# Token rows of the second-to-last stored pair gathered instead of multiplied in, in a fused attention and expert kernel on one core

## The chip, the core and the metric

The kernel runs on one core of a Trainium2 chip. The metric is device time in microseconds, the median of several executions. The kernel before takes 277.7 us (three runs, 277.69 to 277.87). Its times below come from one further execution, taken with the profiler: 277.88 us as timed, of which the profile's span covers 276.1 us, with a granted TensorE clock of 0.998.

The engines are TensorE (PE; its weight loads are listed as PEld), VectorE (DVE), ScalarE (ACT), GpSimd (POOL), and SyncE (SP), which only issues DMAs here. Each engine takes its instructions in the order of the program and stops at a semaphore wait.

## What is computed

Two blocks with a residual each, over 16 batches of 128 tokens with 256 features (2048 tokens):

```
x = x + xattn(layernorm(x), ctx)        # per batch: causal 128 keys + 128 context keys
    h      = layernorm(x);  normed = rmsnorm(h) * norm_w;  pool = [normed, ctx]
    attn   = softmax(mask((normed Wq)(pool Wk)^T / 16))
    alpha  = sigmoid(h Wg + b)
    result = (1 - alpha) * h + alpha * (attn pool)
x = x + ffn(layernorm(x))               # 8 experts, 512 token slots each, top_idx
    for e in 0..7:  rows = layernorm(x)[top_idx[:, e]]                 # 512 x 256
                    out[top_idx[:, e]] += (gelu(rows W1[e] + b1) W2[e] + b2) * combine_w
```

All of it is float32. The large products are made in three passes over a high and a low part (`x_hi`, `x_lo`, `w_hi`, `w_lo`), each held in TensorE's fp32r format.

## The kernel before, in words

**First stage, attention.** The 16 batches are worked in 8 pairs (0 to 7). Every engine runs `attention(p)` once per pair. PE makes the logits, the gate product, the transposes of the probabilities (L1228) and the product with the values (L1244). DVE masks the logits (L901), forms the difference to h (L849), mixes it with the gate (L857, called `mix`), adds the residual to get `x2` (L864), and makes the statistics for the second layernorm. POOL adds x + h ahead of time (`x_plus_h`, L494), makes `normed` (L453) and the inverse root (`rstd`, L471). ACT writes the normalised rows `xn2` (L620). SP stores `x2` to the output (L383) and `xn2` to the table `token_rows` in DRAM.

**Second stage, experts.** For expert e the 512 rows of its slots are gathered from `token_rows` by four indirect DMAs of 128 rows each, which POOL issues (tiles 0 to 3). PE transposes them into two PSUM banks (`ps_xT`), ACT copies them out as `x_hi` (L712), DVE forms `x_lo` (L1021). Then come 8 up products and 8 down products, with gelu on ACT (L731, L732) and its low part on DVE (L1073). While expert e runs, ACT and DVE also split the next expert's weights (L737, L1078). DVE further makes four slot totals per expert (L1052: which slots name the same token), which need the table `seen`. POOL writes `seen` once, after the gathers for expert 1 (L533): a memset (L554) and four selects (L557).

**The seam between the two.** Expert 0 must not wait until the last pairs' rows have gone to DRAM and come back. So its rows come in two parts that are summed in `ps_xT`:

- rows of the first pairs are stored, gathered (`gather_first_rows`, L473), and added by a product with the identity (`early_rows`, L1256). Rows of the late pairs stand as zeros in the table at that time, so that the gather brings zeros for them.
- rows of the late pairs are multiplied in from SBUF by one-hot matrices (`late_rows`, L1264), once with their high and once with their low part. A one-hot matrix (128 x 512) per late batch says which slot wants which token; DVE makes them during the attention stage (`one_hot`, L881).

`EARLY_PAIRS` (L54) is the number of pairs that go by gather. In the kernel before it is 5, so pairs 5, 6 and 7 go by one-hot products: 6 one-hot matrices and 24 products of 128 x 512. The operands are in three slots: `late_hi[0]`, `late_lo[0]` for pair 5 (in the storage of M, free by then), slot 1 for pair 6 (in that of the gate weight), slot 2 for pair 7.

The zeros would be lost if a late pair's rows were stored before the first gathers have read the table. SP therefore waits for all four of them (L400, L401) before it stores the late pairs, and after these come the last list of indices (L407), `x2` of pair 7 (L383) and the two halves of pair 7's rows (L393). POOL's gathers for expert 1 wait until all these stores have landed (L550, L551).

## Time and profile before

| | kernel before |
|---|---|
| median of 3 runs | 277.7 us |
| profiled execution | 277.88 us, span 276.1 us |
| PE busy | 266.3 us (96%) |
| DVE busy | 222.7 us (81%) |
| ACT busy | 180.1 us (65%) |
| POOL busy | 161.7 us (59%) |
| attention stage ends, first rows of expert 0 transposed | about 83.4 us |
| chain that ended last, by engine | PE 81%, DVE 8%, issue 4%, POOL 3%, ACT 2%, DMA 1% |

Times in the rows are microseconds from the start of the span. Busy time does not count waits. A row of the timeline shows the start, the duration from the first start to the last end, the engine, the line, the operation with its output and inputs, and in brackets the idle time ahead of it with what ended it. Consecutive instructions of an engine overlap by some 0.1 us, since the next starts while the last is draining.

### The profile page before, as it was taken

How to read it: one execution, taken by the hardware profiler on the slowest of the kernel's cores; microseconds unless marked ns; L12 is line 12 of the kernel's file. 1: busy time of each engine (PE TensorE's matmuls, PEld its weight loads, DVE VectorE, ACT ScalarE, POOL GpSimd, SP SyncE). 2: the span in 40 equal slices, each digit the busy share in tenths (PEclk: the TensorE clock that was granted, in tenths of full speed). 3: DMA queues.
4: the chain of work that ended last, by engine and by line, in shares of the span. 5: the costliest groups of instructions: out<-in, count | busy, mean ns of one | idle time of the engine just before them, and what ended most of it. 6: DMA issues, size and time to landing. Idle time of an engine off the chain costs nothing.

```text
span 276.1 us, 5494 instructions
## 1 busy us (share of the span) xinstructions
PE 266.3 (96%) x1698; PEld 237.0 (86%) x1698; DVE 222.7 (81%) x526; ACT 180.1 (65%) x341; POOL 161.7 (59%) x153
## 2 busy tenths in 40 slices
PE   6899999999989999999999999999999999999992
PEld 2689899999866989989899899899899899999992
DVE  1988999899986599978878797797887979777552
ACT  2688899886767765766666658567575675763540
POOL 4475766656835945647556457655645746604555
PEclk9999999999999999999999999999999999999999
DMA  6993258496564755635554544654446451100021
GB/s 199 358 275 100 87 143 226 129 260 225 160 197 131 286 153 157 198 117 170 154 200 147 142 141 140 188 174 138 153 133 199 155 156 69 57 21 33 34 78 69
DMA packets 30293, 42.45 MB, mean 154 GB/s; under 512 B 5251, under 2 KB 24015, under 8 KB 30148
## 3 DMA queue, kind: packets, MB, share of 16 engines
q1 hardware_dynamic: 25392, 30.00, 34.7%
q0 software_dynamic: 4608, 12.24, 14.9%
q8 instruction: 8, 0.13, 0.2%
q14 instruction: 9, 0.07, 0.1%
q10 hardware_dynamic: 276, 0.00, 0.1%
HBM read 33.54 MB, written 9.24 MB: 155 GB/s over the span
## 4 chain that ended last, share of the span: by engine, by line
PE 81%; DVE 8%; issue 4%; POOL 3%; ACT 2%; DMA 1%; DVEq 0%; POOLq 0%; ACTq 0%
PE bank L1155 22%; PE bank L1157 22%; PE bank L1156 22%; PE bank L1199 3%; PE bank L1244 3%; PE bank L1296 2%; PE bank L1315 1%; PE bank L1319 1%; PE bank L1316 1%; DMA x_all<-in_x_dram 1%; POOL out_dram L546 1%; DVE bn L754 1%; PE bank L1151 1%; PE bank L1228 1%; PE bank L1164 1%
## 5 line engine op out<-in xcount | busy, mean ns | idle before, releaser
L731 ACT ACTIVATE keysT<-bank,biasT 128x512 f32<-128x512 f32 x63 | 43.5, 690 | 65.4 <-PE bank L1157 55.0
L546 POOL DMA_INDIRECT out_dram<-h,sidx x32 | 38.5, 1205 | 37.5 <-DVE h L1045 30.5
L537 POOL DMA_INDIRECT x_all<-out_dram,idx_all x32 | 39.4, 1232 | 24.3 <-DMA out_dram<-h,sidx 16.8
L1155 PE MATMUL bank<-x_hi,w_hi 128*128 128x512 f32 (+1 forms) x114 | 45.2, 397 | 0.0
L1157 PE MATMUL bank<-x_hi,w_lo 128*128 128x512 f32 (+1 forms) x114 | 44.2, 388 | 0.0
L1156 PE MATMUL bank<-x_lo,w_hi 128*128 128x512 f32 (+1 forms) x114 | 44.1, 387 | 0.0
L533 POOL DMA_INDIRECT x_all<-token_rows,idx_all x28 | 29.8, 1066 | 19.2 <-DVE factor L1096 8.7
L1052 DVE SCALAR_TENSOR_TENSOR junk<-idx_rows,idx_f,normed 128x512 bf16<-128x512 bf16 (+1 forms) x32 | 38.6, 1206 | 3.0 <-POOL normed L557 3.0
L1078 DVE TENSOR_TENSOR w_lo<-w_raw,w_hi 128x512 fp32r<-128x512 f32 x56 | 38.4, 685 | 0.0
L1157 PE MATMUL bank<-w_hi,g_lo 128*128 128x256 f32 x128 | 36.2, 283 | 0.0
L1156 PE MATMUL bank<-w_lo,g_hi 128*128 128x256 f32 x128 | 36.2, 283 | 0.0
L1155 PE MATMUL bank<-w_hi,g_hi 128*128 128x256 f32 x128 | 36.1, 282 | 0.0
L1073 DVE TENSOR_TENSOR g_lo<-keysT,g_hi 128x512 fp32r<-128x512 f32 x32 | 22.1, 690 | 17.1 <-ACT g_hi L732 17.1
L737 ACT CAST w_hi<-w_raw 128x512 fp32r<-128x512 f32 x56 | 34.7, 619 | 0.0
L1157 PEld LDWEIGHTS bank<-x_hi,w_lo 128*128 128x128 f32 x114 | 21.4, 188 | 4.8
L1155 PEld LDWEIGHTS bank<-w_hi,g_hi 128*128 128x128 f32 x128 | 24.4, 190 | 1.3
L1156 PEld LDWEIGHTS bank<-w_lo,g_hi 128*128 128x128 f32 x128 | 24.4, 190 | 1.2
L1157 PEld LDWEIGHTS bank<-w_hi,g_lo 128*128 128x128 f32 x128 | 24.4, 190 | 0.0
L1155 PEld LDWEIGHTS bank<-x_hi,w_hi 128*128 128x128 f32 x114 | 21.5, 189 | 2.8 <-ACT g_hi L732 0.4
L1156 PEld LDWEIGHTS bank<-x_lo,w_hi 128*128 128x128 f32 x114 | 21.6, 189 | 2.4
L732 ACT ACTIVATE g_hi<-bank,biasT 128x512 fp32r<-128x512 f32 x32 | 21.8, 682 | 0.0
L1157 PE MATMUL bank<-w_hi,gateT_lo 128*128 128x256 f32 x64 | 18.0, 282 | 0.0
(172 smaller groups left out, 713.1 us busy)
## 6 DMA issues: line engine op xcount, KB each, us to landing
w_raw<-in_L_ffn_W_dram SPq DMA_DIRECT2D x32, 512.0 KB
idx_rows<-in_L_ffn_top_idx_dram SPq DMA_DIRECT2D x8, 256.0 KB, 4.1
out_dram<-x SPq DMA_DIRECT2D x8, 256.0 KB, 3.0
hn_cnat<-in_ctx_dram SPq DMA_DIRECT2D x7, 256.0 KB, 2.8
token_rows<-xn SPq DMA_DIRECT2D x7, 256.0 KB, 2.2
hn_cnat<-in_L_ffn_b_dram SPq DMA_DIRECT2D x1, 1024.0 KB, 6.6
x_all<-in_x_dram SPq DMA_DIRECT2D x3, 256.0 KB, 4.6
x_all<-in_x_dram SPq DMA_DIRECT2D x1, 768.0 KB, 8.3
```

What stands on the lines that cost most here:

```text
L533: g.indirect_dma_start(xg[:, s, t, :], None, rows_dram, list_of(e, t)).then_inc(xg_in[s], 16)
L537: g.indirect_dma_start(accg[:, t, :], None, flat, list_of(e, t)).then_inc(acc_in[t], 16)
L546: g.indirect_dma_start(flat, idx(sidx[:, t:t + 1].bitcast(U32), 0), newrow[:, t, :], None, bounds_check=N - 1, oob_is_err=False).then_inc( ...
L731: a.activation(g32[:, f % NG, :], ps_up[f % 2][:, :], ACT.Gelu_apprx_tanh, bias=bias)
L732: a.activation(g_hi[f % NG], ps_up[f % 2][:, :], ACT.Gelu_apprx_tanh, bias=bias).then_inc(g_rdy, 1)
L737: a.copy(w_hi[:, 1 - s, col], w_raw[:, col]).then_inc(whi_rdy, 1)
L1052: v.scalar_tensor_tensor(junk[:, :], rows_by_expert[:, ds(e, 1), :].rearrange("p a c -> p (a c)"), idx_f[:, ds(t * NE + e, 1)], seen[:, t, ...
L1073: v.tensor_tensor(g_lo[f % NG], g32[:, f % NG, :], g_hi[f % NG].bitcast(F32), ALU.subtract)\
L1078: v.tensor_tensor(w_lo[:, 1 - s, col], w_raw[:, col], w_hi[:, 1 - s, col].bitcast(F32), ALU.subtract).then_inc(wlo_rdy, 1)
L1155: t_.matmul(dst, lhs_hi, rhs_hi, start=first, stop=False)
L1156: t_.matmul(dst, lhs_hi, rhs_lo, start=False, stop=False)
L1157: return t_.matmul(dst, lhs_lo, rhs_hi, start=False, stop=last_one)
```

## The change

Pair 5 joins the pairs that are stored and gathered: `EARLY_PAIRS` becomes 6, so there are 4 one-hot matrices instead of 6, and two slots of operands instead of three. The cast and the subtraction that made pair 5's high and low part are gone, and so are its 8 products. Two products with a matrix of zeros (`junk`) now open the accumulation in `ps_xT` instead. They stand in the last pair behind the transposes of the probabilities.

The four first gathers wait for pair 5's store. All of them now stand behind the last pair's x + h on POOL: tiles 0 and 1 ahead of `rstd` of pair 6, tile 2 ahead of the last pair's first `rstd`, tile 3 ahead of its second. On PE the products of the seam are in a new order, and DVE makes the low part of the last pair's first batch ahead of the last shift.

```diff
-    EARLY_PAIRS = NPAIR - 3
+    EARLY_PAIRS = NPAIR - 2
...
-        late_hi = [M_hi[:, :, :], gateT_hi[:, :, :], hnT_hi[:, 0, :, :]]
-        late_lo = [M_lo[:, :, :], gateT_lo[:, :, :], hnT_lo[:, 0, :, :]]
+        late_hi = [gateT_hi[:, :, :], hnT_hi[:, 0, :, :]]
+        late_lo = [gateT_lo[:, :, :], hnT_lo[:, 0, :, :]]
...
-                    for late in (LAST - 2, LAST - 1):
-                        sp.wait_ge(xn_rdy, 2 * late + 2)
-                        sp.dma_start(rows_v[:, 2 * late:2 * late + 2, 0:H], xn2[:, late % 2, :, :])\
-                            .then_inc(xn_out[late % 2], 16)
+                    sp.wait_ge(xn_rdy, 2 * r + 2)
+                    sp.dma_start(rows_v[:, 2 * r:2 * r + 2, 0:H], xn2[:, r % 2, :, :]).then_inc(xn_out[r % 2], 16)
...
                 if is_last(p):
-                    gather_first_rows(range(1, NT))
+                    gather_first_rows(range(2))
...
-                if p == LAST - 1:
-                    gather_first_rows(range(1))
...
             for b in range(2):
+                gather_first_rows(range(2 + b, 3 + b))
                 last_rstd(b)
...
-                if is_last(p):
-                    act.wait_ge(xn_rdy, 2 * p - 2)
-                    act.wait_ge(q_mm, NPAIR)
-                    a.copy(late_hi[0], xn2[:, s, :, :]).then_inc(late_hi_rdy, 1)
                 for b in range(2):
...
-                    a.copy(late_hi[1], xn2[:, 1 - s, :, :]).then_inc(late_hi_rdy, 1)
+                    a.copy(late_hi[0], xn2[:, 1 - s, :, :]).then_inc(late_hi_rdy, 1)
...
-                a.activation(late_hi[2][:, b, :], x2[:, 1, b, :], ACT.Identity, bias=shift2[:, 1, b:b + 1],
+                a.activation(late_hi[1][:, b, :], x2[:, 1, b, :], ACT.Identity, bias=shift2[:, 1, b:b + 1],
...
-                    if not is_last(p):
+                    if not isinstance(p, int):
...
                 v.reciprocal(rinv[:, :], rsum[:, :]).then_inc(ri_rdy, 1)
-                if is_last(p):
-                    dve.wait_ge(late_hi_rdy, 1)
-                    dve.wait_ge(xn_rdy, 2 * LAST - 2)
-                    v.tensor_tensor(late_lo[0], xn2[:, s, :, :], late_hi[0].bitcast(F32), ALU.subtract)\
-                        .then_inc(late_lo_rdy, 1)
...
             last_pair_variance(1)
-            dve.wait_ge(late_hi_rdy, 2)
+            dve.wait_ge(late_hi_rdy, 1)
...
-            v.tensor_tensor(late_lo[1], xn2[:, 1 - last_s, :, :], late_hi[1].bitcast(F32), ALU.subtract)\
+            v.tensor_tensor(late_lo[0], xn2[:, 1 - last_s, :, :], late_hi[0].bitcast(F32), ALU.subtract)\
                 .then_inc(late_lo_rdy, 1)
+            def last_pair_low(b):
+                dve.wait_ge(late_hi_rdy, 2 + b)
+                dve.wait_ge(last_xn[b], 1)
+                v.tensor_tensor(late_lo[1][:, b, :], xn_last[:, b, :], late_hi[1][:, b, :].bitcast(F32),
+                                ALU.subtract).then_inc(late_lo_rdy, 1)
+            last_pair_low(0)
             last_pair_shift(1)
...
-            for b in range(2):
-                dve.wait_ge(late_hi_rdy, 3 + b)
-                dve.wait_ge(last_xn[b], 1)
-                v.tensor_tensor(late_lo[2][:, b, :], xn_last[:, b, :], late_hi[2][:, b, :].bitcast(F32),
-                                ALU.subtract).then_inc(late_lo_rdy, 1)
+            last_pair_low(1)
...
-                    pe.wait_ge(log_rdy, 2 * NPAIR - 1)
-                    pe.wait_ge(late_hi_rdy, 1)
-                    for b in range(2):
-                        late_rows(0, b, late_hi, first=b == 0)
                 pe.wait_ge(exp_rdy, 2 * p + 2)
...
                 if is_last(p):
-                    early_rows(range(1))
+                    pe.wait_ge(log_rdy, 2 * NPAIR - 1)
+                    for k in range(KH):
+                        t_.matmul(ps_xT[k][:, :], junk[:, 0:P], junk[:, :], start=True, stop=False)
...
-            def late_rows(n, b, part, first=False):
+            def late_rows(n, b, part):
...
-                              start=first, stop=False)
+                              start=False, stop=False)
             each_pair(pe, attention)
-            early_rows(range(1, NT))
-            for n in range(2):
-                if n:
-                    pe.wait_ge(late_hi_rdy, n + 1)
-                    for b in range(2):
-                        late_rows(n, b, late_hi)
-                pe.wait_ge(late_lo_rdy, n + 1)
+            early_rows(range(2))
+            pe.wait_ge(late_hi_rdy, 1)
+            for b in range(2):
+                late_rows(0, b, late_hi)
+            early_rows(range(2, 3))
+            pe.wait_ge(late_hi_rdy, 2)
+            late_rows(1, 0, late_hi)
+            pe.wait_ge(late_lo_rdy, 1)
+            for b in range(2):
+                late_rows(0, b, late_lo)
+            early_rows(range(3, NT))
+            for k in range(KH):
+                cols = slice(k * P, (k + 1) * P)
+                pe.wait_ge(late_hi_rdy, 3)
+                t_.matmul(ps_xT[k][:, :], late_hi[1][:, 1, cols], onehot[:, 3, :], start=False, stop=False)
                 for b in range(2):
-                    late_rows(n, b, late_lo)
-            for b in range(2):
-                pe.wait_ge(late_hi_rdy, 3 + b)
-                late_rows(2, b, late_hi)
-            for k in range(KH):
-                for b in range(2):
-                    pe.wait_ge(late_lo_rdy, 3 + b)
-                    last = t_.matmul(ps_xT[k][:, :], late_lo[2][:, b, k * P:(k + 1) * P], onehot[:, 4 + b, :],
+                    pe.wait_ge(late_lo_rdy, 2 + b)
+                    last = t_.matmul(ps_xT[k][:, :], late_lo[1][:, b, cols], onehot[:, 2 + b, :],
```

POOL at the seam, kernel before (from the last `rstd` inside the loop of pairs; `rstd ... 128x2` is a pair's, `128x1` one batch's of pair 7; `x_all<-token_rows` are gathers, the first four for expert 0, the last for expert 1):

```order
L471 TENSOR_TENSOR rstd<-var_eps,half_neg 128x2 [waits x2_var_eps_ready]
L481 DMA x_all<-token_rows,idx_all 128x264 [waits xn2_stored0,late_rows_zeroed,xn2_stored1,idx_loaded,combine_copied]
L494 TENSOR_TENSOR x_plus_h<-x_all,h 128x512 [waits x2_shift_ready,h_ready]
L481 DMA x_all<-token_rows,idx_all 128x264 [waits xn2_stored0,late_rows_zeroed,xn2_stored1,idx_loaded,combine_copied]
L481 DMA x_all<-token_rows,idx_all 128x264 x2
L471 TENSOR_TENSOR rstd<-var_eps,half_neg 128x2 [waits x2_var_eps_ready]
L523 TENSOR_TENSOR rstd<-var_eps,half_neg 128x1 [waits x2_var_eps_ready] x2
L533 DMA x_all<-token_rows,idx_all 128x264 [waits xn2_stored1,x2_stored1,x2_stored0,xn2_stored0]
```

The same place on POOL in the changed kernel:

```order
L469 TENSOR_TENSOR rstd<-var_eps,half_neg 128x2 [waits x2_var_eps_ready]
L492 TENSOR_TENSOR x_plus_h<-x_all,h 128x512 [waits x2_shift_ready,h_ready]
L479 DMA x_all<-token_rows,idx_all 128x264 [waits xn2_stored0,late_rows_zeroed,xn2_stored1,idx_loaded,combine_copied]
L479 DMA x_all<-token_rows,idx_all 128x264
L469 TENSOR_TENSOR rstd<-var_eps,half_neg 128x2 [waits x2_var_eps_ready]
L479 DMA x_all<-token_rows,idx_all 128x264 [waits xn2_stored0,late_rows_zeroed,xn2_stored1,idx_loaded,combine_copied]
L519 TENSOR_TENSOR rstd<-var_eps,half_neg 128x1 [waits x2_var_eps_ready]
L479 DMA x_all<-token_rows,idx_all 128x264 [waits xn2_stored0,late_rows_zeroed,xn2_stored1,idx_loaded,combine_copied]
L519 TENSOR_TENSOR rstd<-var_eps,half_neg 128x1 [waits x2_var_eps_ready]
L530 DMA x_all<-token_rows,idx_all 128x264 [waits xn2_stored1,x2_stored1,x2_stored0,xn2_stored0]
```

The last pair's x + h has moved ahead of the gathers, and the gathers of tiles 2 and 3 now stand each in front of one of the last pair's inverse roots.

PE in the last pair, kernel before (behind the gate product; `w_hi` holds the one-hot matrices, `M_hi` pair 5's high part, L1228 transposes the probabilities, L1261 is a gathered tile):

```order
L1219 MATMUL bank<-ident,bias_rows 128x64 [waits bias_loaded]
L1268 MATMUL bank<-w_hi,M_hi 128x512 [waits one_hot_ready,late_rows_high,masked_logits_max]
L1268 MATMUL bank<-w_hi,M_hi 128x512
L1268 MATMUL bank<-w_hi,M_hi 128x512 [waits one_hot_ready]
L1268 MATMUL bank<-w_hi,M_hi 128x512
L1228 MATMUL bank<-ident,setup_or_probs 128x128 [waits exp_done]
L1228 MATMUL bank<-ident,setup_or_probs 128x128 x3
L1261 MATMUL bank<-ident,x_all 128x128 [waits first_rows_gathered0]
L1261 MATMUL bank<-ident,x_all 128x128
L1244 MATMUL bank<-normed,setup_or_probs 128x256 [waits diff_ready,normed_ready,probsT_ready]
```

The same place on PE in the changed kernel:

```order
L1211 MATMUL bank<-ident,bias_rows 128x64 [waits bias_loaded]
L1216 MATMUL bank<-ident,setup_or_probs 128x128 [waits exp_done]
L1216 MATMUL bank<-ident,setup_or_probs 128x128 x3
L1225 MATMUL bank<-junk 128x512 [waits masked_logits_max]
L1225 MATMUL bank<-junk 128x512
L1234 MATMUL bank<-normed,setup_or_probs 128x256 [waits diff_ready,normed_ready,probsT_ready]
```

The transposes of the probabilities follow the gate product directly, and tile 0 of the gathered rows has moved behind the product with the values.

## Rows read from the trace of the kernel before

**Rows 1.** busy time of each engine (instructions) in one stretch of expert 0.

```profile
100.00:110.00 10.00, 10.00 (x65) 8.99 (x64) 9.93 (x21) 6.38 (x12) 4.42 (x5) 1.00 0.52 144
```

**Rows 2.** chain of waits, in order of time: start, us, what; the seam.

```profile
83.45 0.59 ACT x_hi L712
```

**Rows 3.** timeline of PE, end of attention.

```profile
71.94 1.20 PE L1268 MATMUL bank<-w_hi,M_hi 128*128 128x512 f32 x4
72.98 0.60 PE L1228 MATMUL bank<-ident,setup_or_probs 128*128 128x128 f32 x4
...
74.26 0.70 PE L1244 MATMUL bank<-normed,setup_or_probs 128*128 128x256 f32 x2 [0.23 <-ACT setup_or_probs L653]
```

**Rows 4.** timeline of ACT, last pair.

```profile
69.44 1.09 ACT L620 ACTIVATE xn<-x,shift,rstd 128x256 f32<-128x256 f32 x2 [1.30 <-DVE shift L888]
70.56 0.62 ACT L642 CAST M_hi<-xn 128x512 fp32r<-128x512 f32 x1
...
73.62 0.59 ACT L653 COPY setup_or_probs<-bank 128x512 f32<-128x512 f32 x1 [1.44 <-PE bank L1228]
```

**Rows 5.** timeline of DVE, pairs 6 and 7.

```profile
63.75 0.48 DVE L883 TENSOR_SCALAR w_hi<-idx_rows,tok_f 128x512 fp32r<-128x512 f32 x1
...
70.92 1.52 DVE L857 SCALAR_TENSOR_TENSOR diff<-setup_or_probs,diff 128x512 f32<-128x512 f32 x1
...
75.12 0.67 DVE L948 TENSOR_TENSOR M_lo<-xn,M_hi 128x512 fp32r<-128x512 f32 x1
75.71 0.48 DVE L966 SCALAR_TENSOR_TENSOR diff<-bank,rinv,h 128x256 f32<-128x256 f32 x1
...
77.03 0.15 DVE L888 SCALAR_TENSOR_TENSOR shift<-mv,rstd 128x2 f32<-128x2 f32 x1
```

**Rows 6.** all instructions of L857: duration in ns, min/median/max.

```profile
L857 DVE SCALAR_TENSOR_TENSOR diff<-setup_or_probs,diff x7: 682/684/1518, 25.9 to 70.9; 128x512 f32<-128x512 f32 x7
```

**Rows 7.** timeline of POOL, last pair and after.

```profile
69.35 1.21 POOL L481 DMA_INDIRECT x_all<-token_rows,idx_all  x1 [0.20 <-issue]
70.58 1.30 POOL L494 TENSOR_TENSOR x_plus_h<-x_all,h 128x512 f32<-128x512 f32 x1
...
74.83 0.95 POOL L481 DMA_INDIRECT x_all<-token_rows,idx_all  x1 [0.30 <-issue]
75.80 0.73 POOL L471 TENSOR_TENSOR rstd<-var_eps,half_neg 128x2 f32<-128x2 f32 x1
78.05 0.56 POOL L523 TENSOR_TENSOR rstd<-var_eps,half_neg 128x1 f32<-128x1 f32 x1 [1.51 <-DVE var_eps L985]
...
85.05 1.04 POOL L533 DMA_INDIRECT x_all<-token_rows,idx_all  x1 [3.86 <-DMA token_rows<-qT]
...
92.42 2.32 POOL L557 TENSOR_SCALAR_AFFINE_SELECT normed<-normed 128x512 bf16<-128x512 bf16 x4
```

**Rows 8.** timeline of SP, DMAs issued at the seam.

```profile
77.94 0.87 SPq L404 DMA_DIRECT2D token_rows<-xn  x2
...
79.41 0.46 SPq L383 DMA_DIRECT2D out_dram<-x  x1
80.02 2.17 SPq L393 DMA_DIRECT2D token_rows<-qT  x2
```

**Rows 9.** DMA issues of 77 to 86 us: KB each, median us to landing.

```profile
token_rows<-xn SPq DMA_DIRECT2D x2, 256.0 KB, 2.4
...
out_dram<-x SPq DMA_DIRECT2D x1, 256.0 KB, 4.0
token_rows<-qT SPq DMA_DIRECT2D x2, 128.0 KB, 2.9
```

**Rows 10.** timeline of DVE in expert 0.

```profile
94.88 1.24 DVE L1052 SCALAR_TENSOR_TENSOR junk<-idx_rows,idx_f,normed 128x512 bf16<-128x512 int32 x1 [2.98 <-POOL normed L557]
...
104.86 1.28 DVE L1021 TENSOR_TENSOR x_lo<-bank,x_hi 128x512 fp32r<-128x512 f32 x2
```

**Rows 11.** timeline of the weight loads, start of expert 1.

```profile
106.19 0.19 PEld L1319 LDWEIGHTS bank<-x_lo,w_hi 128*128 128x128 f32 x1 [0.16 <-issue]
```

More of the change, by code:

```diff
@@ L386, in _ @@
                     load_ctx(r + 3)
-                if r == EARLY_PAIRS - 2:
+                if r == EARLY_PAIRS - 3:
                     sp.wait_ge(xh_rdy, r + 1)
```

## The prediction

> **What bounds the kernel now.** I read the table of stretches first. While the experts run, PE has no gap: in the stretch from 100 to 110 us it is busy 10.00 of 10.00 us, and DVE 9.93 [rows 1]. So what the seam gives or takes reaches the end in full, if PE still starts expert 0 at the seam's pace and nobody makes it wait later. The chain of waits says when expert 0's rows are ready: ACT starts to copy them at 83.45 [rows 2]. That is the time the change works on. Then I looked for whoever has no slack in expert 0, and it is DVE. It stands still for 2.98 us until POOL has written `seen` (its first slot total starts at 94.88), and from there it works without a pause to the low parts of expert 1's rows, L1021, which end at 104.86 + 1.28 = 106.14 [rows 10]. PE's weight load that needs them starts at 106.19, after 0.16 us of idling [rows 11]. PE itself doesn't stall there, since the matmuls in front of it still run, so the slack of this second chain is 0.05 to 0.15 us; I take 0.1. Read backwards it is: x_lo of expert 1, DVE's block of work, `seen` (selects end at 92.42 + 2.32 = 94.74), POOL's memset and gathers for expert 1 from 85.05, and these waited 3.86 us for the last store of pair 7's rows to land [rows 7]. The forecast is decided on this chain, not on the one that the change shortens.
>
> **PE, ACT and DVE in the last pair.** The four products between the gate product and the transposes go: 72.98 - 71.94 = 1.04 us [rows 3]. ACT's cast L642 (0.62, of which some 0.5 is its place in the queue) goes with them, so the second exponential ends near 71.65 and doesn't hold the transposes back [rows 4]. The evacuation L653 moves from 73.62 to about 72.6 and the product with the values from 74.26 to 73.2. The two products with zeros lie in the gap that PE has while ACT evacuates (0.23 us idle before 74.26, and tile 0 has left it) [rows 3, 4]: two at the 0.3 us of a 512-column product (1.20 for four) fit into the 0.6 us of the evacuation, cost 0.
>
> On DVE, L857 took 1.52 us in the last pair and 0.684 in the median of seven [rows 5, 6]. It began at 70.92, while POOL's x + h ran from 70.58 to 71.88 [rows 7]. 71.88 + 0.6 is its end, so it looks as if it worked only after POOL was done. In the new order x + h stands ahead of the gathers and starts near 69.3, as soon as pair 5's shift is out. It ends by 70.6, before L857, and 0.83 us come back. L948 (75.12 to 75.71, 0.59) goes as well [rows 5]. DVE would be free for the last pair's difference L966 at 75.71 - 0.83 - 0.59 = 74.29; the values come about 1.04 earlier than before, near 74.5. I take 74.5: 1.2 us won. The one-hot matrices of pairs 5 and 6 (0.4 each by their place in the queue, 63.75 [rows 5]) leave DVE too. PE is dense there, so this moves nothing but pair 5's statistics, 0.4 us sooner.
>
> The Trainium skill bears on L857 ("SBUF — State Buffer", the section on the single rule): a DVE instruction with two SBUF inputs and a POOL instruction that reads SBUF take turns for a whole instruction. The two rows fit it. If that rule were not the cause, L857 would stay at 1.52 and the sum below would be 0.8 us worse.
>
> **POOL: the gathers.** Here is what the change costs. Before, tile 0 was issued at 69.35 and tile 3 at 74.83 [rows 7]. Now the first one waits for pair 5's rows. ACT wrote them from 69.44 for 1.09 us, to 70.5 [rows 4]; with 0.4 from the one-hot matrix, 70.1. Their store takes 2.4 us to land [rows 9], POOL 0.3 us from a landing to the next gather (SP's last store was issued at about 81.8, its row's end 80.02 + 2.17 less an issue of some 0.4 [rows 8], and landed 2.9 later at 84.7; POOL starts at 85.05). That makes 72.8 for tile 0, 3.4 us later than before. Two gathers of 1.05 + 0.3 end at 75.2, `rstd` of pair 6 (0.73) at 75.95. DVE wants it for the shift that stood 1.32 us behind L966 (75.71 to 77.03 [rows 5]): at 75.8 in the new kernel. It waits 0.2 and goes on at 76.0. Tile 2 runs from 76.15 to 77.2. The last pair's first `rstd` was issued 1.02 us behind that shift (78.05 [rows 7]), and now runs from 77.2 to 77.8. Tile 3 follows at 77.95, which is 3.1 us later than 74.83.
>
> **PE at the seam.** SP's first store behind the gathers was issued 3.11 us after tile 3 (77.94 [rows 8] less 74.83), so tile 3 is there at 81.05. PE then has one tile (four blocks, 0.5) and three products of 512 columns (1.20 for four [rows 3], so 0.9): ACT starts at 82.5 instead of 83.45 [rows 2]. Expert 0 begins 0.95 us sooner. The DVE part alone would allow 82.2.
>
> **SP and POOL behind it.** SP's queue is what ties the two chains. It may not store pair 6 before tile 3 is there. From 81.05 it issues pair 6's store (0.44, half of 0.87), the last list (79.41 - 77.94 - 0.87 = 0.60), `x2` (0.5) and pair 7's first half (0.4), so its second half is issued at 82.95 [rows 8]. Before, that was at 81.8, when it waited for DVE and not for the queue. So it is 1.15 us later. It lands 2.9 us after its issue [rows 9], or more, because the four DMAs ahead of it (256 + 256 + 256 + 128 KB) are now all issued within 2 us; the store of `x2` took 4.0 in the crowd before [rows 9], which bounds it at +1.1. I take 0.15 of that. POOL starts expert 1's gathers 1.3 us late, at 86.35, and `seen` is ready at 96.05 in place of 94.74.
>
> **The sum.** DVE's block moves with `seen`: x_lo is ready at 107.45. Less the slack of 0.1, PE is 1.2 us later than before at the start of expert 1, whatever it won at 82.5. (It stalls in two steps: first for the low part of gelu 3, which DVE makes right behind the first slot total, then for x_lo.) From there PE is dense in both kernels and nothing is given back. 277.88 + 1.2 = 279.1 for an execution like the profiled one, which is 0.18 above the median of the three; against that median it is 278.9.
>
> **Bounds.** The least delay: the store lands so soon that gathers never hold up DVE's shift. Then the shift is at 75.8, tile 3 at 77.7, landing as before at 2.9: +0.7, 278.4. The most: L857 keeps its 1.52 (+0.8) and the last store takes 4.0 (+0.9): 280.6. Indirect DMAs cost 0.95 to 1.21 each in the rows [rows 7], so three of them carry 0.8 between the ends; I took the middle.
>
> **Rivals.** *Faster:* the seam alone decides and POOL's and SP's later queue is covered. Then PE keeps its 0.95 us, or 1.25 if tile 3 comes sooner: 276.4 to 276.8. For it: the chain of the profile runs through DVE and PE at the seam, never through SP. Against it: DVE's 2.98 us wait for `seen` is in the rows, and x_lo has no slack. It needs the last store issued by 81.8, hence tile 3 by 76.8; POOL would have to issue it ahead of an inverse root whose input DVE has at about 76.9.
>
> *No change:* the last store catches up most of the way. Its landing in the crowd before (2.9 us with a list and an `x2` ahead) may already hold 0.5 to 1 us of queueing that doesn't grow. With 1.15 reduced to 0.3 to 0.6 the result is 277.7 to 278.2.
>
> *Slower by more:* pair 5's store lands late. It is the front of DVE's chain as well: each 0.1 us later than 72.5 moves tiles 0 and 1, pair 6's `rstd`, DVE's shift and everything behind it, with no slack (DVE waits 0.2 already). A landing of 4.0, the largest of the rows [rows 9], instead of 2.4 gives +1.6: 280.5. Against it: SP issues nothing else for some microseconds ahead of it.
>
> A rule that bears on this landing: by the Trainium skill ("DMA: Bandwidth & Descriptors", the anatomy of one DMA), about 2.0 us of a DMA is fixed and mostly the receipt of the last write. With 2.0 for pair 5's store in place of 2.4 the delay would be 0.2 us less, not more, since DVE sets the rest.
>
> **Chances.** Slower along this chain, 278.3 to 279.6: 0.57. Slower by more: 0.15. No change: 0.15. Faster: 0.13. A measurement of this kernel tells a change above about 0.2%, 0.55 us, from none. So slower 0.72, same 0.15, faster 0.13. The time of the likeliest case is 278.9. The range 277.4 to 280.3 leaves out most of the faster case and the upper third of the last.
>
> **What would show it.** In the new trace: L857 of the last pair at 0.68; the product with the values near 73.2; the first gather near 72.8 with an idle time ended by a store, and DVE's shift of pair 6 ended by POOL's `rstd`; tile 3 issued near 78; ACT's x_hi near 82.5; SP's last row store issued near 83 and POOL's first gather for expert 1 near 86.3. The first slot total would start near 96.2, with DVE waiting 4 us or more for `seen`. PE, gapless from 84 us on before, would now show idle time between 96 and 108 us, ended by DVE. The forecast is wrong if that idle time is missing, or if the last store is issued at 82 or sooner.

## The result and the profile after

The changed kernel takes 284.1 us (four runs, 282.31 to 285.45), against 277.78 us for the kernel before in the same session (four runs, 277.69 to 279.12): ratio 1.0206, 95% interval 1.0169 to 1.0242. Slower was right. The size was not: 278.9 was predicted, with a range that ended at 280.3.

Page of the changed kernel, the profiled execution of 285.42 us: span, busy times, and the row of the slot totals, whose last field is the idle time ahead of them:

```profile
span 283.6 us, 5473 instructions
PE 269.9 (95%) x1692; PEld 238.5 (84%) x1692; DVE 221.8 (78%) x523; ACT 179.8 (63%) x340; POOL 161.1 (57%) x153
L1044 DVE SCALAR_TENSOR_TENSOR junk<-idx_rows,idx_f,normed 128x512 bf16<-128x512 bf16 (+1 forms) x32 | 38.5, 1203 | 6.5 <-POOL normed L554 6.5
```

DVE now waits 6.5 us for `seen`, where it waited 2.98 [rows 10]. But that isn't the whole loss, and it pays to cut the span at two instructions that both kernels have: the last pair's logits on PE (start: 68.49 before, 72.95 after) and the first product with `x_hi` (84.19 before, 88.23 after). Kernel before:

```profile
68.49 1.89 PE L1199 MATMUL bank<-keysT,qT 128*128 128x256 f32 x8
84.19 0.47 PE L1315 MATMUL bank<-x_hi,w_hi 128*128 128x512 f32 x1 [0.30 <-ACT x_hi L712]
```

Changed kernel:

```profile
72.95 1.89 PE L1191 MATMUL bank<-keysT,qT 128*128 128x256 f32 x8
88.23 0.47 PE L1307 MATMUL bank<-x_hi,w_hi 128*128 128x512 f32 x1
```

| | before | after | difference |
|---|---|---|---|
| start of span to last pair's logits | 68.49 | 72.95 | +4.46 |
| logits to first product with x_hi ("seam") | 15.70 | 15.28 | -0.42 |
| from there to the end ("rest") | 191.91 | 195.37 | +3.46 |
| span | 276.1 | 283.6 | +7.5 |

**The first part** lies ahead of everything that the change touches. PE at the start, changed kernel (start, us, instruction, idle time ahead):

```profile
1.33 4.02 PE L1122 MATMUL bank<-junk 128*128 128x512 bf16 x9 [1.33 <-POOL junk L425]
7.05 2.08 PE L1131 MATMUL bank<-setup_or_probs 128*128 128x256 f32 x4 [1.70 <-DMA setup_or_probs<-in_L_xattn_k_w_dram]
9.78 1.91 PE L1131 MATMUL bank<-setup_or_probs 128*128 128x256 f32 x4
```

and in the kernel before:

```profile
6.12 1.13 PE L1139 MATMUL bank<-setup_or_probs 128*128 128x256 f32 x4 [0.77 <-DMA setup_or_probs<-in_L_xattn_k_w_dram]
8.25 1.03 PE L1139 MATMUL bank<-setup_or_probs 128*128 128x256 f32 x4
```

The k weights landed 0.93 us later, and then the same four products took 2.08 us instead of 1.13, the next four 1.91 instead of 1.03: about half speed, as the clock's lower level of 1.2 GHz in place of 2.4 would give, although the column of the granted clock says 1.00 there. It lasts until about 16.5 us, and with the 0.93 us off it costs some 3.5 us.

**The other two parts** are the change. To compare with the rows of before, take 4.46 off each time (68.49 against 72.95 for the last pair's logits). SP, changed kernel:

```profile
74.62 0.36 SPq L396 DMA_DIRECT2D token_rows<-xn  x1
86.16 0.36 SPq L403 DMA_DIRECT2D token_rows<-xn  x1
86.57 0.48 SPq L343 DMA_DIRECT2D idx_rows<-in_L_ffn_top_idx_dram  x1
87.09 0.45 SPq L383 DMA_DIRECT2D out_dram<-x  x1
87.58 0.96 SPq L393 DMA_DIRECT2D token_rows<-qT  x2
```

POOL, the same stretch:

```profile
77.79 1.21 POOL L479 DMA_INDIRECT x_all<-token_rows,idx_all  x1 [2.96 <-DMA token_rows<-xn]
80.27 0.78 POOL L469 TENSOR_TENSOR rstd<-var_eps,half_neg 128x2 f32<-128x2 f32 x1
83.06 1.12 POOL L479 DMA_INDIRECT x_all<-token_rows,idx_all  x1 [0.17 <-issue]
92.81 1.00 POOL L530 DMA_INDIRECT x_all<-token_rows,idx_all  x1 [7.60 <-DMA token_rows<-qT]
```

Four rows of the chain of waits (start, us, what) show what lies between a store's issue and the gather that waits for it. "issue" is POOL starting its DMA after the landing:

```profile
74.62 2.25 DMA token_rows<-xn
76.93 0.86 issue
88.09 3.88 DMA token_rows<-qT
92.10 0.71 issue
```

POOL's gathers for expert 1 start at 92.81 - 4.46 = 88.35, against 85.05 [rows 7]: 3.3 us later, not 1.3. DVE (the mix of the last pair is L850 now, the difference L954, pair 6's shift L881):

```profile
75.38 0.69 DVE L850 SCALAR_TENSOR_TENSOR diff<-setup_or_probs,diff 128x512 f32<-128x512 f32 x1
79.07 0.48 DVE L954 SCALAR_TENSOR_TENSOR diff<-bank,rinv,h 128x256 f32<-128x256 f32 x1
81.09 0.16 DVE L881 SCALAR_TENSOR_TENSOR shift<-mv,rstd 128x2 f32<-128x2 f32 x1 [0.62 <-POOL rstd L469]
102.57 1.19 DVE L1044 SCALAR_TENSOR_TENSOR junk<-idx_rows,idx_f,normed 128x512 bf16<-128x512 int32 x1 [6.52 <-POOL normed L554]
```

And PE, which in the kernel before stands still for 0.2 to 0.4 us at a time in the seam and nowhere from 85 us on:

```profile
77.73 0.70 PE L1234 MATMUL bank<-normed,setup_or_probs 128*128 128x256 f32 x2 [0.24 <-ACT setup_or_probs L646]
81.60 1.21 PE L1251 MATMUL bank<-ident,x_all 128*128 128x128 f32 x8 [1.88 <-DMA x_all<-token_rows,idx_all]
100.78 1.09 PE L1288 MATMUL bank<-ident,x_all 128*128 128x128 f32 x8 [0.66 <-DMA x_all<-token_rows,idx_all]
104.43 0.39 PE L1147 MATMUL bank<-w_hi,M_lo 128*128 128x256 f32 x1 [1.17 <-DVE gateT_lo L1065]
113.16 1.09 PE L1311 MATMUL bank<-x_lo,w_hi 128*128 128x512 f32 x2 [0.47 <-DVE x_lo L1013]
```

The first gathered tiles in the kernel before:

```profile
77.13 1.41 PE L1261 MATMUL bank<-ident,x_all 128*128 128x128 f32 x8 [0.27 <-DMA x_all<-token_rows,idx_all]
```

PE stands still in the seam for 1.88 us for the first gathered tiles. Behind it, it waits for the low part of gelu 3 (1.17 us) and for x_lo of expert 1 (0.47 us, and 0.90 us for the weight load), as forecast from the late `seen`. The wait of 0.66 us for expert 1's gathered rows is not in the forecast. It doesn't set the end here, since DVE's chain is later still, but after_sp below is left with it.

### The profile page after: what moved, and what is told of

Its sections match the earlier page's. It is cut to its first block, busy times and chain, and to the rows that moved or that the text cites. A ratio compares the mean times of both kernels' runs of the same rounds, so it can differ in the third digit from the quotient of the medians.

```text
span 283.6 us, 5473 instructions
## 1 busy us (share of the span) xinstructions
PE 269.9 (95%) x1692; PEld 238.5 (84%) x1692; DVE 221.8 (78%) x523; ACT 179.8 (63%) x340; POOL 161.1 (57%) x153
## 4 chain that ended last, share of the span: by engine, by line
PE 74%; DVE 6%; POOL 6%; DMA 5%; issue 4%; ACT 2%; SPq 1%; DVEq 0%; POOLq 0%; ACTq 0%
PE bank L1147 20%; PE bank L1149 19%; PE bank L1148 19%; PE bank L1191 4%; PE bank L1234 2%; DMA setup_or_probs<-in_L_xattn_k_w_dram 2%; PE bank L1288 2%; DVE junk L1044 2%; POOL x_all L530 2%; DMA token_rows<-qT 1%; PE bank L1131 1%; PE bank L1311 1%; PE bank L1143 1%; POOL x_all L479 1%; DMA x_all<-token_rows,idx_all 1%
## 5 line engine op out<-in xcount | busy, mean ns | idle before, releaser
L534 POOL DMA_INDIRECT x_all<-out_dram,idx_all x32 | 38.8, 1213 | 23.5 <-DMA out_dram<-h,sidx 16.0
L1147 PE MATMUL bank<-w_hi,M_lo 128*128 128x256 f32 x64 | 18.1, 283 | 1.2 <-DVE gateT_lo L1065 1.2
```

The lines of the kernel that those rows point to most:

```text
L534: g.indirect_dma_start(accg[:, t, :], None, flat, list_of(e, t)).then_inc(acc_in[t], 16)
L1147: t_.matmul(dst, lhs_hi, rhs_hi, start=first, stop=False)
```

## The experiments

All times are medians in us; "seam + rest" is from the last pair's logits to the end of the span in the profiled execution, which leaves the start out (before: 207.61, after: 210.65). Executions of the kernel before itself fall into two groups, near 277.7 and near 279.1; before_cold below points to what sets them apart. How many fall in the upper one changed from session to session (4 of 17 to 20 of 35), so the ratios of different sessions can't be set against each other, and I read medians beside them. The expectations call two ideas by name. "Chain theory": the last row store holds POOL, POOL's late `seen` holds DVE, and DVE holds PE. "Port theory": an instruction of DVE stands still while one of POOL runs.

| run | median (runs) | ratio, 95% | seam + rest |
|---|---|---|---|
| after_again | 280.96 (5) | 1.0106, 1.0085 to 1.0126 | 210.67 |
| before_warm | 278.04 (12) | 0.9991, 0.9975 to 1.0007 | 207.62 |
| after_warm | 281.44 (5) | 1.0120, 1.0095 to 1.0145 | 210.99 |
| after_seen | 279.26 (11) | 1.0041, 1.0022 to 1.0060 | 208.67 |
| after_sp | 278.34 (12) | 0.9995, 0.9973 to 1.0017 | 208.24 |
| after_seen_wait | 278.83 (12) | 1.0010, 0.9987 to 1.0033 | 208.64 |
| after_seen_wait_sp | 279.10 (12) | 1.0021, 0.9998 to 1.0044 | 208.47 |
| before_xh | 278.78 (12) | 1.0000, 0.9978 to 1.0021 | 208.07 |
| before_cold | 279.36 (12) | 1.0042, 1.0021 to 1.0064 | 208.21 |
| before_sp | 277.86 (12) | 0.9975, 0.9958 to 0.9992 | 207.55 |
| before_probs | 278.02 (12) | 0.9984, 0.9967 to 1.0000 | 207.59 |
| after_sp_b2 | 278.09 (12) | 0.9994, 0.9975 to 1.0013 | 208.50 |
| after_sp_b2_fill | 278.15 (12) | 1.0003, 0.9982 to 1.0025 | 207.88 |
| after_cold | 282.96 (6) | 1.0199, 1.0150 to 1.0248 | 210.96 |

**after_again**: the changed kernel as it is, once more.

> The changed kernel unaltered, for more executions. Start theory: its executions fall into groups, set by when the first weights land; where TensorE idles about 1.7 us after its warm-up products, the next 9 us of products run at half speed and the execution takes about 285.4; where it idles 0.8 us, it takes 281 to 282.5. The kernel before shows the same two starts, more rarely. Rival, the change is the whole cause: all executions of the changed kernel lie at 282 to 285.5 and none of the kernel before leaves 277.7 to 277.9.

280.96 (280.64 to 281.14). All five lie at or just under the faster of the two groups that I expected (281 to 282.5); neither the slower one near 285.4 nor the rival's 282 to 285.5 was seen. PE starts the setup at 6.24 at full speed, and the last pair's logits start at 68.23. So the slow start doesn't belong to the changed kernel as such, and the change's own cost is about 3.1 us (210.67 - 207.61). Its first gather for expert 1:

```profile
88.16 1.00 POOL L530 DMA_INDIRECT x_all<-token_rows,idx_all  x1 [7.59 <-DMA token_rows<-qT]
```

**before_warm, after_warm**: 15 warm-up products instead of 9 in either kernel.

```diff
-            keep_warm(9)
+            keep_warm(15)
```

> Kernel before with 15 warm-up products in place of 9, so that TensorE works until about 6.7 us. Start theory: 277.7 to 278.0, all executions within 0.5 us, since the late landing of the first weights no longer meets an idle TensorE. Rival, the start has no part in it: the same spread as the kernel before.

> Changed kernel with 15 warm-up products. Start theory plus the chain over the last row store, POOL and DVE: the profile showed the seam's chain 3.1 us later than before beyond the start's 4.46, so 280.8, narrow. Rival, the change is the whole cause: 282 to 285.5 as without it. My forecast's size for the chain (1.2 us) would give 279.0.

No execution of before_warm lies above 278.44. The difference between the two is 3.4 us, with after_warm 0.6 us above what I expected. The profile of after_warm (mean clock 0.992, as in two more of the five) shows one more way in which a late `seen` costs. Table of stretches, PE alone: busy us (instructions), granted clock, DMA share, GB/s:

```profile
96.00:100.00 4.00, 2.18 (x14) 1.00 0.04 9
100.00:104.00 4.00, 3.93 (x18) 0.66 0.65 210
104.00:108.00 4.00, 4.00 (x26) 0.91 0.55 171
```

After PE has stood still for 1.89 us (98.2 to 100.1, for the low part of gelu 3), the granted clock is 0.50 from about 101.3 to 104.3, its lower level. So the 3.4 us hold some 0.3 us of this fall (seam + rest is 210.99, in after_again 210.67).

**after_seen**: `seen` (memset and selects) is written ahead of POOL's wait for the last store; 15 warm-up products in this and in the runs that follow, where nothing else is said.

```diff
-            for s in range(2):
-                pool.wait_ge(xn_out[s], 16 * (NPAIR // 2) + 16 + 16 * s)
-                pool.wait_ge(x2_out[s], 16 * (NPAIR // 2) + 16)
-            gather_rows(1, 1)
             pool.wait_ge(pv_mm, NPAIR)
             g.memset(seen, 1.0).then_inc(consts, 1)
...
+            for s in range(2):
+                pool.wait_ge(xn_out[s], 16 * (NPAIR // 2) + 16 + 16 * s)
+                pool.wait_ge(x2_out[s], 16 * (NPAIR // 2) + 16)
+            gather_rows(1, 1)
```

> Changed kernel with 15 warm-up products, and POOL writes the table seen ahead of its wait for the last row store instead of behind expert 1's gathers. Chain theory: DVE no longer waits 6.5 us in expert 0, what is left is expert 1's gathered rows, which TensorE needed 0.7 us before they landed; 277.9 to 278.3. Rival, another part of the change costs the time (stores, gathers or products at the seam): stays within 0.5 us of the kernel with 15 warm-up products alone.

DVE no longer waits for `seen`, and 2.2 us of the 3.4 come back. That is less than the 3.1 to 3.5 that I expected, since the memset collides with DVE in the seam:

```profile
81.21 1.68 DVE L1006 TENSOR_SCALAR qT<-x,rstd,shift 128x256 f32<-128x256 f32 x1
```

```profile
80.94 1.79 POOL L547 MEMSET normed<- 128x2048 bf16 x1
```

L1006 took 0.41 us in the changed kernel and 1.68 here: it ends (82.89) right behind POOL's memset (80.94 + 1.79 = 82.73). x_hi is 1.2 us later. The Trainium skill ("SBUF — State Buffer", Who interferes with whom) says that a DVE instruction in a mode that uses both port pairs, which tensor_scalar can enter, and a POOL instruction exclude each other for whole instructions. The trace fits that. It doesn't show in which mode L1006 ran: its 0.41 us is also what a tensor_tensor of this size takes (L1000, 0.42).

**after_sp**: `seen` stays where the change has it, and SP issues pair 7's two halves ahead of the last list and of `x2`, for which POOL's gathers no longer wait.

```diff
                 sp.wait_ge(x2_rdy, r + 1)
+                if r == LAST:
+                    for b in range(2):
+                        sp.wait_ge(last_xn[b], 1)
+                        sp.dma_start(rows_v[:, 2 * r + b, 0:H], xn_last[:, b, :]).then_inc(xn_out[r % 2], 16)
+                    sp.wait_ge(onehot_rdy, NB - EARLY)
+                    load_lists(IDX_PARTS - 1)
                 sp.dma_start(out_v[:, 2 * r:2 * r + 2, :], x2[:, r % 2, :, :]).then_inc(x2_out[r % 2], 16)
...
                 pool.wait_ge(xn_out[s], 16 * (NPAIR // 2) + 16 + 16 * s)
-                pool.wait_ge(x2_out[s], 16 * (NPAIR // 2) + 16)
             gather_rows(1, 1)
+            for s in range(2):
+                pool.wait_ge(x2_out[s], 16 * (NPAIR // 2) + 16)
```

> Changed kernel with 15 warm-up products; SP issues both halves of pair 7's rows directly behind pair 6's store, then the last list, then x2, and POOL waits for the x2 stores only behind expert 1's gathers. Chain theory: last row store issued about 1 us sooner and landing in 3 us in place of 3.9, so expert 1's gathers, seen, DVE's block and the end all 1.9 us sooner than with the warm-up alone: 279.4. Rival, the order and the crowd on SP's queue do not matter and the landing is fixed: at most 1 us, 280.4 or more. Rival, the chain doesn't end in seen: no change, 281.4.

278.34: 3.1 us of the 3.4 are gone, more than the 2 us expected. By seam + rest it is 2.4 us of the change's own 3.1 (210.67 to 208.24); 0.6 us are left, and PE's wait for the gathered rows (0.71 us) is what the profile shows for them. POOL's first gather for expert 1, the first row that PE waits for behind the seam, and the two row stores' time from issue to landing:

```profile
85.44 1.09 POOL L530 DMA_INDIRECT x_all<-token_rows,idx_all  x1 [4.69 <-DMA token_rows<-qT]
```

```profile
96.40 1.09 PE L1289 MATMUL bank<-ident,x_all 128*128 128x128 f32 x8 [0.71 <-DMA x_all<-token_rows,idx_all]
```

```profile
DMA to landing us min/median/max: 2.1/2.1/2.1
```

In the changed kernel the same two stores took

```profile
DMA to landing us min/median/max: 3.5/3.7/3.9
```

So a 128 KB store lands in 2.1 us with 256 KB of pair 6's rows issued 0.5 us ahead of it, and in 3.5 to 3.9 us with a list and an `x2` (256 KB each) in between. What is issued ahead of it makes the difference of up to 1.8 us. The Trainium skill ("DMA: Bandwidth & Descriptors", Anatomy of one DMA) puts the fixed part of a DMA that GpSimd issues at about 2.0 us, with the time of the bytes on top. By its sum the 256 KB of pair 5's store would take 2.6 us, an estimate (the prediction took the fixed part alone); the store landed in 2.25. These stores are issued by SP, and before_sp below has the same 128 KB landing in 1.7 us, so for them the fixed part is smaller than that.

**after_seen_wait, after_seen_wait_sp**: `seen` ahead of POOL's wait, but behind a wait for the last low part (so that it can't collide with L1006); the second one with SP's order too.

```diff
             pool.wait_ge(pv_mm, NPAIR)
+            pool.wait_ge(late_lo_rdy, 3)
             g.memset(seen, 1.0).then_inc(consts, 1)
```

> Changed kernel with 15 warm-up products; POOL writes seen ahead of its wait for the last row store, but only once DVE has made the last low part at the seam. Port theory: L1006 at 0.41 in place of 1.68 us and x_hi 1.2 us sooner than with seen written at once. Chain theory for the end: expert 1's gathered rows come as late as there and now bound TensorE, so 279.2 again, with TensorE idle 1.4 us ahead of their transposes. Rival, the seam alone counts once seen is out of the way: 278.0.

> Both edits together: seen early but behind DVE's last low part, and pair 7's rows stored ahead of the last list and x2. Chain theory: neither seen nor expert 1's rows bind, the seam's gain of 0.4 us stays: 277.2 to 277.6, the first version below the kernel before. Rival, some third wait of expert 0 takes over: 278.0 or more.

The port theory holds in both: the tensor_scalar is back at 0.41 us. In after_seen_wait_sp:

```profile
81.02 0.41 DVE L1008 TENSOR_SCALAR qT<-x,rstd,shift 128x256 f32<-128x256 f32 x1
```

The times are a miss in both. after_seen_wait has 278.83 instead of 279.2, and its profiled execution (279.69) has PE waiting 0.16 us for expert 1's rows instead of 1.4: it lost the time in the seam (16.46 us), where the granted clock is 0.50 from 79 to 82 us. The pair doesn't add up: together 279.10, SP's order alone 278.34. `seen` in front costs POOL about 2 us (gathers for expert 1 at 87.55 instead of 85.44), and what then ends last is no longer `seen` but the gathered rows: PE waits 0.89 us at 96.59 for them. Of after_seen_wait_sp's 12 executions 4 lie near 280.1, with a mean clock of 0.991.

**before_xh**: the kernel before, with the last pair's x + h ahead of all four gathers.

```diff
                 if is_last(p):
-                    gather_first_rows(range(1, NT))
+                    gather_first_rows(range(NT))
...
-                if p == LAST - 1:
-                    gather_first_rows(range(1))
```

> Kernel before with 15 warm-up products and only the last pair's x + h moved ahead of all four first gathers. Port theory: L857 of the last pair takes 0.68 in place of 1.52 us. The last pair's difference then starts when the values are there, 0.25 us sooner; the end doesn't move (277.9 to 278.1), since DVE's block in expert 0 starts at seen, which is as late as before. Rival, what is won at the seam reaches the end: 277.2 to 277.8. Rival, L857 is not held by POOL: stays 1.52.

The mix of the last pair takes 0.76 us instead of 1.52 [rows 5], with nothing else moved on DVE: what held it was POOL's x + h. But tile 0 is gathered 1.6 us later (2.47 us behind the last pair's logits, 0.84 in before_warm), and stands in front of the product with the values on PE, so the gain turns into a wait. DVE:

```profile
71.36 0.76 DVE L855 SCALAR_TENSOR_TENSOR diff<-setup_or_probs,diff 128x512 f32<-128x512 f32 x1
76.60 0.48 DVE L964 SCALAR_TENSOR_TENSOR diff<-bank,rinv,h 128x256 f32<-128x256 f32 x1 [1.12 <-PE bank L1242]
```

PE:

```profile
74.89 0.71 PE L1259 MATMUL bank<-ident,x_all 128*128 128x128 f32 x4 [0.86 <-DMA x_all<-token_rows,idx_all]
```

The seam is 16.14 us (15.70), the rest 191.93 (191.91): 0.44 us lost in this execution, and the median is 0.74 us above before_warm. So I was right on L857 and wrong on the time, which I had expected unchanged.

**before_probs**: in the kernel before, the transposes of the probabilities ahead of pair five's four products.

```diff
-                    pe.wait_ge(log_rdy, 2 * NPAIR - 1)
-                    pe.wait_ge(late_hi_rdy, 1)
-                    for b in range(2):
-                        late_rows(0, b, late_hi, first=b == 0)
...
                 if is_last(p):
+                    pe.wait_ge(log_rdy, 2 * NPAIR - 1)
+                    pe.wait_ge(late_hi_rdy, 1)
+                    for b in range(2):
+                        late_rows(0, b, late_hi, first=b == 0)
                     early_rows(range(1))
```

> The kernel before with 15 warm-up products, and in the last pair the transposes of the probabilities ahead of pair five's four products on PE; nothing else is moved. Theory of the seam (expert 0 starts with the last pair's statistics, through DVE): the values come 0.9 us sooner, L857 keeps its 1.5 us and DVE comes to the difference at 74.9 instead of 75.5, so x_hi is 0.5 to 0.6 us sooner than 83.66 and the time 277.5. Rival (DVE is the bound there and takes nothing sooner, or PE has the four products back at the end of the seam): 278.0 as before_warm.

278.02, seam 15.72: the rival holds. L857 still takes 1.54 and pair five's low part 0.67, and DVE comes to the difference at 75.65 as before. In the seam PE waits for DVE. That an earlier product with the values counts once L857 is short and the low part gone, as in the changed kernel, follows from this but was not run by itself.

**before_sp**: SP's order in the kernel before.

> The kernel before with 15 warm-up products and SP's order of after_sp: rows of pairs 5 and 6, both halves of pair 7, the last list, x2. Theory (expert 0 of the kernel before is bound by PE alone, and the last store already lands 2.3 us behind its issue because it waits for DVE and not for the queue): SP's order gives POOL at most 0.3 us and PE nothing: 277.8 to 278.3, the same as before_warm (278.04). Rival (SP's order shortens something else, the crowd of 80 to 98 us): 0.5 us or more faster, 277.5 or less, and then what after_sp won was not the changed kernel's own queue.

277.86 and seam + rest 207.55: the same as before_warm. Pair 7's two stores, from issue to landing:

```profile
DMA to landing us min/median/max: 1.7/1.7/1.7
```

So SP's order isn't a gain of its own; it repairs what the change broke. (The ratio, 0.9975, comes from the 20 of 35 executions of the kernel before that were in the upper group in that session.)

**before_cold, after_cold**: 5 warm-up products.

```diff
-            keep_warm(9)
+            keep_warm(5)
```

> The kernel before with 5 warm-up products instead of 9, so that PE stands idle for about 2.5 us (0.77 before) until the k weights are there. Theory of the start: an idle PE of 1.7 us or more ahead of the setup products leaves the products behind it at half speed until about 16.5 us, as in the first execution of the changed kernel (12 query products 0.21 apart, M_rows 2.08 us for four), and everything behind is 3.5 us later: 281 to 282, in all of its executions. Rival: the half speed has nothing to do with the idle time (it is only the later landing of the weights in some executions): the products start when the weights land, 277.7 to 278.4 as for 15 warm-up products.

> The changed kernel with 5 warm-up products instead of 9. In before_cold every execution was 1.2 us or more above the kernel before's lower group (products at half speed to about 10 us). Theory: the first session's times of the changed kernel (282.31, 282.78, 285.42, 285.45) are its own 280.9 and a slow start of either 1.3 or 4.5 us; then all executions here lie near 282.2, and single ones near 285.4. Rival (the slow start is of that session or the first build and not of the idle PE): 280.9 to 281.2 as in after_again.

PE at the start of before_cold:

```profile
6.19 2.08 PE L1139 MATMUL bank<-setup_or_probs 128*128 128x256 f32 x4 [2.55 <-DMA setup_or_probs<-in_L_xattn_k_w_dram]
8.91 1.29 PE L1139 MATMUL bank<-setup_or_probs 128*128 128x256 f32 x4
```

All 12 executions lie between 278.94 and 281.34, at the upper group's time or more, so products at half speed behind an idle PE are the likely cause of that group (none of its executions was profiled). But they run slow only to about 10 us, and the last pair's logits start at 69.39, 0.9 us late, not 3.5 as I expected. (The rest is 0.6 us longer too in this execution, 192.51; I found no cause.) In the changed kernel it gives 282.44 to 283.13 in four executions, 284.05, and one of 286.36. That resembles the first session's times (282.31, 282.78, 285.42, 285.45), of which only the 285.42 was profiled. What makes the slow stretch last until 16 us in some executions I haven't found.

**after_sp_b2, after_sp_b2_fill**: after_sp with the 1 MB load of the output biases later; and with five products with zeros in PE's gap ahead of the first tiles.

```diff
             sp.wait_ge(pv_mm, NPAIR)
+            sp.wait_ge(wlo_rdy, 3)
             row_broadcast(b2_bc, b2.rearrange("e h -> (e h)")).then_inc(b2_in, 16)
...
             each_pair(pe, attention)
+            for n in range(5):
+                t_.matmul(ps_xT[n % KH][:, :], junk[:, 0:P], junk[:, :], start=False, stop=False)
             early_rows(range(2))
```

(The last two lines with a + are in after_sp_b2_fill alone.)

> after_sp, and the 1 MB load of the output biases waits for the third low part of expert 1's weights: issued near 91.8 instead of 86.7, behind the gathers for expert 1. In after_sp PE stood idle 0.71 us ahead of 96.40 for the last of these gathers (issued 89.38, landed about 96.2) and 3.70 of 4.00 us busy before that. Theory (the gathers share the DMA engines with that load): they land 2 us or more sooner, the idle time goes, 277.5 to 277.8, and the executions near 279.2 with a clock of 0.992 go too. Rival (the gathers are bound by themselves or by the weights): the idle time stays, 278.3.

> after_sp_b2 with five more products with zeros on PE ahead of the first gathered tile, where PE stood idle for 1.16 to 1.5 us. Theory: the executions of the changed kernel and its variants near 279.5 (3 of 12 in after_sp, 3 of 12 in after_sp_b2, mean clock 0.992) come from the idle time that the later gathers leave in the seam: the profile of after_sp_b2 shows the granted clock at 0.50 from 79 to 82 us and a seam of 16.46 us instead of 15.32. With the gap filled none of the 12 executions has a mean clock under 0.995, and all lie at 277.8 to 278.5. Rival (that clock falls for another reason): 2 to 4 of 12 near 279.5 again. A price of up to 0.1 us where a zero product stands in front of tile 0.

PE's wait at 96.4 is gone in both, but the median of after_sp_b2 is 278.09, only 0.25 us less and not the 277.5 to 277.8 expected, and the executions near 279.5 are still there. The profiled one (279.60) caught what three of its 12 have. PE alone: busy us (instructions), granted clock, DMA share, GB/s:

```profile
77.00:78.00 1.00, 0.69 (x4) 1.00 0.49 135
78.00:79.00 1.00, 0.51 (x4) 0.94 0.00 0
79.00:80.00 1.00, 0.90 (x4) 0.50 0.49 135
80.00:81.00 1.00, 1.00 (x4) 0.50 0.00 0
```

The seam takes 16.46 us there instead of 15.32 in after_sp. With the gap filled,

```profile
75.53 1.24 PE L1265 MATMUL bank<-junk 128*128 128x512 bf16 x5
76.93 0.71 PE L1253 MATMUL bank<-ident,x_all 128*128 128x128 f32 x4 [0.16 <-DMA x_all<-token_rows,idx_all]
```

no execution of 12 has a mean clock under 0.995, and the slowest is 278.82 (three lie above the 278.5 expected). In after_sp, after_sp_b2, after_seen_wait and after_seen_wait_sp 15 of 48 were at 0.993 or less, against 1 of 109 executions of the kernel before in these sessions. So the later gathers, which leave PE idle in the seam, bring this risk. The idle time alone doesn't decide it: the profile of after_sp has PE idle for 1.16 and 0.58 us at the same place with the clock at 1.00 throughout, that of after_sp_b2 for 1.24 and 0.49 us with the fall. And 0 of 12 against 3 of 12 in the same kernel without the filling could still be chance. The median doesn't move by it (278.15). No version here beats the kernel before's lower group (277.7).

## Why the prediction was wrong

The direction and the chain were right, two terms of it were too small, and a third part came from outside the change. The first two are enough for the miss: without the slow start the changed kernel takes 281.0, above the range that ended at 280.3. All times relative to the last pair's logits:

| step | predicted | measured (after) |
|---|---|---|
| product with the values, sooner | 1.04 | 0.99 |
| mix of the last pair, shorter | 0.83 | 0.83 |
| first gather (tile 0), from the logits | 4.3 | 4.84 |
| DVE waits for pair 6's `rstd` | 0.2 | 0.62 |
| tile 3 issued | 9.46 | 10.11 |
| x_hi sooner | 0.95 | 0.41 |
| last row store issued later | 1.15 | 1.75 |
| its landing, and POOL's start behind it, longer | 0.15 | 1.55 |
| POOL's gathers for expert 1 later | 1.3 | 3.30 |
| seam + rest | +1.2 | +3.04 |

**Right**: the steps on PE, ACT and DVE in the last pair; that POOL's x + h held L857 (before_xh shows it by itself); that SP's queue ties the two chains; that `seen` carries the delay to DVE (after_seen takes that wait away and gets 2.2 us back), and DVE to PE with next to no slack; that PE is dense again behind it.

**The step "first one waits for pair 5's rows", 0.55 us too small.** I took 0.3 us from a landing to the next gather. It is 0.9 us: pair 5's store was issued at 74.62 and landed at 76.87, and POOL's gather started at 77.79. The 0.3 came from a sum that fitted by accident: I put the last store of the kernel before at 2.9 us to landing [rows 9] and 0.3 us to POOL, but the 2.9 is the median of two unlike halves. Both halves together, and the last one (issued at 81.9) by itself:

```profile
DMA to landing us min/median/max: 2.3/2.9/3.5
DMA to landing us min/median/max: 2.3/2.3/2.3
```

It was 2.3 and 0.85. For the last store the sum was right either way. For the new wait on the path it was not, and the 0.6 us pass through `rstd`, DVE's shift, tiles 2 and 3 and SP's whole list: tile 3 is 0.65 us late, and x_hi gains 0.41 instead of 0.95.

**The step "It lands 2.9 us after its issue, or more ... I take 0.15", 1.4 us too small.** The landing went from 2.3 to 3.9 us. In the kernel before, SP waited for DVE between the two halves of pair 7, so that the second half was issued at 81.9, 2.5 us behind `x2` (79.41, landed 4.0 later), when the transfers ahead of it were partly done. In the changed kernel all five DMAs are issued within 2.4 us, `x2` only 1.0 us ahead of the last one, and I read the longer landing as a wait for the bytes of the others. I had even bounded it at +1.1 by the crowd's 4.0 us [rows 9], and then took the number near the lower end. after_sp shows both halves of the SP term at once: with the row stores first, the last one is issued 1.0 us sooner behind the logits and lands in 2.1 us, and 3.1 us come back.

With the two numbers put right (0.55 and 1.4 more) the prediction's own sum gives 277.88 + 1.2 + 1.95 = 281.0; after_again measured 280.96. The two corrections were read from the changed kernel's trace, so this shows that the steps account for the loss, not that the sum could have forecast it.

**A wait that the prediction doesn't have.** Expert 1's gathered rows come late as well, and PE waits 0.66 us for them. It cost nothing extra as long as DVE's chain ended later, but it is the next limit: 0.71 us in after_sp, 0.89 us in after_seen_wait_sp.

**The start, +1.3 or +4.5 us.** It is not in the prediction at all, and the change doesn't need it: the same changed kernel had none in the five executions of after_again. before_cold makes one like the smaller in the kernel before by taking warm-up products away, and single executions of the kernel before had 282.25 and 282.46. That the changed kernel seems to have had one or the other in all four executions of the first session (by their times; one was profiled, and the 285.45 has a mean clock of 0.971, so it may be something else) stays unexplained.

**The rivals.** "Faster" and "no change" fell with the issue of the last store at 83.6 instead of 81.8. "Slower by more" named pair 5's store as late; it landed in 2.25 us. The chain was later by another link: 0.9 us instead of 0.3 from that landing to the gather, and the last store's landing.

## What to carry to other kernels

When a change makes one queue issue later, price two things: the later issue, and that its transfers are now issued back to back, so that the last one can land later behind its issue (3.9 us instead of 2.3 here). Store what somebody waits for first, and the rest behind it. A landing isn't the end of a wait: for an indirect gather add the waiting engine's own start (0.9 us here), and take both numbers from one and the same DMA, never a median of unlike ones. Before a difference of 1% or more is put down to a change, cut both traces at an instruction that they share, and see whether the part ahead of the change is the same.

## What the hardware showed that I had not expected

- Products at half speed from 7 to 16.5 us, with a granted clock of 1.00 in that column: at the start of this kernel the column doesn't show such a stretch, and the duration of the products does (2.08 instead of 1.13 us for four).
- A fall of the clock in the middle of the kernel behind 1.2 to 1.9 us of idle PE. In 15 of 48 executions of four versions the mean clock was 0.993 or less; the two of them that were profiled have the fall in the seam, 1.15 us longer. With five products with zeros in the gap it was in none of 12.
- A POOL memset of 1.79 us held a DVE tensor_scalar of 0.41 us until it was over (1.68 us).
- From the landing of a store to the start of an indirect gather on POOL that waits for it: 0.92 us for the first gather, 0.84 us for expert 1's.
